# Score tiles and max tiles interleaved by row half in a causal attention kernel

## The chip, the cores and the metric

The kernel runs on one core of a Trainium2 chip. The metric is the device time of one execution in microseconds (us), of which three runs are shown; the profile is of one further execution.

## The reference

A transformer block on x of shape (4, 2048, 256), float32. Sixteen heads of 16 dimensions.

```python
x = x + attention(layernorm(x), Wq, Wk, Wv, Wo)   # rotary Q and K, causal softmax
x = x + ffn(layernorm(x), w1, b1, w2, b2)         # relu, width 1024

scores = einsum('bhqd,bhkd->bhqk', Q, K) / sqrt(16)
scores = where(causal_mask, -inf, scores)
attn = softmax(scores, axis=-1)
out = einsum('bhqk,bhkd->bhqd', attn, V)
```

## The kernel before

Three stages run one after the other. Stage 1 normalizes x, projects Q, K and V, applies the rotation, and stores Q and K as float16 high and low parts and V in scratch memory. Stage 3 scales the attention output, projects it, and runs the feed-forward net. Stage 2, the attention, is where the change lies.

Stage 2 works on 16 groups (4 batches x 4 groups of 4 heads; index `i`). A group has 40 steps (`STEPS`, L49): for each chunk `c` of 512 queries, the key blocks `kb` of 128 keys from 0 to the last that the causal mask leaves. The last four steps of a chunk touch the diagonal (`is_diagonal`, L62); the others, 0, 4, 8 and 12 in chunks 0 to 3, are the full steps, 24 per group. In each step, for each of the 4 heads of the group, a score tile of 128 keys x up to 512 queries is computed (`score_tile`, L716), ScalarE takes its exponential out of PSUM (L869), GpSimd zeroes what lies above the diagonal in diagonal steps (L899), and one step later TensorE multiplies the probabilities with V (`pv_step`, L726, in two parts of half the columns, each of four matmuls that use 32 columns of the array each, float32). ScalarE copies the output bank once per chunk, in the step after the chunk's last (L860); the first value matmul of the next chunk waits for that copy (L733).

The softmax needs each query's maximum before its scores. It is computed half a group of steps ahead (`LAG` = 20 steps, L58), by separate matmuls with queries on the partitions, the max tiles (`max_pair`, L692, matmul L705); VectorE reduces them to maxima. For a tile wholly below the diagonal, one reduce takes the two banks of a pair (L797). For a tile that crosses it, VectorE adds a mask and takes the maximum bank by bank (L804). When a chunk's tiles are through, VectorE makes the row of negated maxima (L812, L817, L822), which travels through scratch memory into the score operand. Every step carries one max tile per head; full steps carry full tiles, diagonal steps carry diagonal ones (`max_tiles`, L72). The last 20 steps of the last group have no max tiles left.

All these matmuls have a contraction of at most 64 rows. Heads 0 and 2 of a group lie in partitions 0 to 63, heads 1 and 3 in partitions 64 to 127 (`HROWS`), for scores and max tiles alike. Below, S0 to S3 and M0 to M3 are the score and max matmuls of heads 0 to 3.

TensorE's order in a step is written out by hand in `iteration` (L754): S0 S1, M0 M1, S2, value part 0, S3, M2 M3, value part 1. Scores use three PSUM banks in turn, so a score waits until ScalarE has read the third score before it (L720). Max tiles use four banks, one per head, so a pair waits until VectorE has read the same pair of the step before (L702, L704): by one wait for both banks, on the pair's first matmul, for a full tile. The value parts wait for all four exponentials of the step before (L737), or for all four of its masks (L735), and ScalarE's first exponential of a step waits for the value parts of two steps before (L866).

Of the kernel before, what the change touches and what calls it, by code (L numbers as in the profile page):

```python
# [46 lines left out]
NP = G // 2  # L47
# [14 lines left out]
def is_diagonal(s):  # L62
    c, kb = STEPS[s]
    return kb >= TPC * c


def diagonals(s):

    return sum(is_diagonal(t) for t in range(s))
# [455 lines left out]
def stage2(nc, x, qk_d, v_d, att_d, rows_d, rinv_d, weight_ds, weights, ops):  # L525
    with ExitStack() as ctx:
# [41 lines left out]
        STEPS_M = NIT * NS  # L568
# [7 lines left out]
        def m_use(t, j):  # L576

            return G * t + j

        def bank_of(use):  # L580

            return M_BANK + use % NM

        def s_bank(s, j):

            return S_BANK + (G * s + j) % SB

        def read_before(i, s, j):

            u = G * s + j  # L590
            last_in_bank = u - SB if u >= SB else max(t for t in range(ST) if t % SB == u) - ST
            return ST * i + last_in_bank + 1

        def crosses_diagonal(qt, kc):
            return kc == qt // TPC
# [93 lines left out]

        @block.tensor  # L690
        def _(pe):
            def max_pair(t, pair):  # L692

                p, use = t // NS % 2, m_use(t, 2 * pair)
                if pair == 0 and t % NS == 0:
                    pe.wait_ge(m_in[p], 128 * (t // NS // 2 + 1))
                qt, kc = MAX_TILES[t % NS]
                w = min(CH, (qt + 1) * P - kc * CH)
                for jj in range(2):
                    rows = slice(HROWS * jj, HROWS * (jj + 1))  # L700
                    if crosses_diagonal(qt, kc):
                        pe.wait_ge(m_read, use + jj + 1)  # L702
                    elif jj == 0:
                        pe.wait_ge(m_read, use + 2)  # L704
                    nc.tensor.matmul(ps[:, bank_of(use + jj), 0:w], mq[rows, p, pair, qt * P:(qt + 1) * P],  # L705
                                     mk[rows, p, pair, kc * CH:kc * CH + w], start=True, stop=True).then_inc(m_ready, 1)

            def filler_pair(p, s, pair):

                qt, kc = MAX_TILES[(s + LAG) % NS]  # L710
                for jj in range(2):
                    rows = slice(HROWS * jj, HROWS * (jj + 1))
                    nc.tensor.matmul(ps[:, M_BANK + 2 * pair + jj], mq[rows, p, pair, qt * P:(qt + 1) * P],
                                     mk[rows, p, pair, 0:CH], start=True, stop=True)

            def score_tile(i, p, s, j):  # L716

                c, kb = STEPS[s]
                q0 = max(0, kb - TPC * c) * P
                pe.wait_ge(p_done, G + read_before(i, s, j))  # L720
                rows = slice(HROWS * (j % 2), HROWS * (j % 2 + 1))
                nc.tensor.matmul(ps[:, s_bank(s, j), q0:CH], ak[rows, p, j // 2, kb * P:(kb + 1) * P],  # L722
                                 aq[rows, p, j // 2, c * CH + q0:(c + 1) * CH], start=True, stop=True
                                 ).then_inc(s_ready, 1)

            def pv_step(i, p, s, part):  # L726

                c, kb = STEPS[s]
                q0 = max(0, kb - TPC * c) * P
                half = (CH - q0) // 2  # L730
                if part == 0:
                    if kb == 0:
                        pe.wait_ge(o_copied, NC * i + c)  # L733
                    if is_diagonal(s):
                        pe.wait_ge(mask_done, G * (NDIAG * i + diagonals(s) + 1))  # L735
                    else:
                        pe.wait_ge(p_done, ST * i + G * s + G + G)  # L737
                cols = slice(q0 + half * part, q0 + half * (part + 1))
                for j in range(G):

                    last = nc.tensor.matmul(ps[32 * j:32 * j + 32, O_BANK, cols], v[:, p, kb, j, :],  # L741
                                            prob[:, s % 2, j, cols], start=kb == 0 and part == 0,
                                            stop=kb == TPC * (c + 1) - 1 and part == 1)
                if part == 1:
                    last.then_inc(pv_done, 1)

            def value_step(i, p, s, part):

                if s > 0:
                    pv_step(i, p, s - 1, part)  # L750
                elif i > 0:
                    pv_step(i - 1, 1 - p, NS - 1, part)

            def iteration(i, p, use):  # L754

                pe.wait_ge(a_in[p], A_DMAS * 16 * (use + 1))
                pe.wait_ge(v_in[p], 16 * (use + 1))
                for s in range(NS):
                    t = NS * i + s + LAG
                    if t == STEPS_M:  # L760
                        pe.wait_ge(m_read, NM + m_use(STEPS_M, 0))
                    if s in CHUNK_START:
                        pe.wait_ge(rows_in[STEPS[s][0]], 16 * ROWS_DMAS * (i + 1))
                    score_tile(i, p, s, 0)
                    score_tile(i, p, s, 1)
                    if t < STEPS_M:
                        max_pair(t, 0)
                    elif is_diagonal(s):
                        filler_pair(p, s, 0)
                    score_tile(i, p, s, 2)  # L770
                    value_step(i, p, s, 0)
                    score_tile(i, p, s, 3)
                    if t < STEPS_M:
                        max_pair(t, 1)
                    elif is_diagonal(s):
                        filler_pair(p, s, 1)
                    value_step(i, p, s, 1)

            for t in range(LAG):
                for pair in range(NP):  # L780
                    max_pair(t, pair)
            for u in range(NIT // 2):
                iteration(2 * u, 0, u)
                iteration(2 * u + 1, 1, u)
            pv_step(NIT - 1, 1, NS - 1, 0)
            pv_step(NIT - 1, 1, NS - 1, 1)
# [492 lines left out]
```

## Time and profile before

| | |
|---|---|
| median of 3 runs | 2129.21 us (2128.51 to 2129.35) |
| profiled execution | 2130.91 us, span 2129.2 us |
| mean granted TensorE clock | 0.973 of full speed |
| TensorE busy | 1996.2 us, 94% |
| VectorE busy | 1909.1 us, 90% |
| ScalarE busy | 1446.1 us, 68% |
| GpSimd busy | 637.3 us, 30% |

The span is the time from the first to the last instruction of the profiled execution. In the rows, PE is TensorE's matmuls, PEld its weight loads, DVE is VectorE, ACT ScalarE, POOL GpSimd. Busy time is a union: instructions that overlap on one engine count once, so a mean duration can be longer than the time from one start to the next.

### The profile page before, as it was taken

The page shows a single profiled execution, that of the slowest core. Times are in us where ns is not written, and L with a number is a line of the kernel's source. Part 1 is how long each engine was busy: PE and PEld are TensorE (multiplying, and loading weights), DVE is VectorE, ACT ScalarE, POOL GpSimd, SP SyncE. Part 2 cuts the span into 40 slices and gives each one's busy share as a digit, 9 for nine tenths or more (in the row PEclk, how much of TensorE's full clock was granted, in tenths as well). Part 3 has the DMA queues.
Part 4 walks back from the last instruction along what each step waited for, and adds up shares of the span by engine and source line. Part 5 has one row for each costly group of instructions (what it writes and reads, how often), then busy time and mean ns, then how long its engine had stood idle before and what let it go on. Part 6 is the DMA issues. An engine that isn't in the chain of part 4 may idle for free. (4 is left out here: it accounts for less than half of the span.)

```text
span 2129.2 us, 53450 instructions
## 1 busy us (share of the span) xinstructions
PE 1996.2 (94%) x19104; PEld 797.7 (37%) x19104; DVE 1909.1 (90%) x4039; ACT 1446.1 (68%) x3092; POOL 637.3 (30%) x1265
## 2 busy tenths in 40 slices
PE   5787499999999999999999999999999979999998
PEld 3444023232322223232232322323323246667776
DVE  8999799999999999999999999999999247777775
ACT  5665078888888888888888888888888823333222
POOL 7999512120222212121121211212212123333331
PEclk9999589999999999999999999999999989999999
DMA  5657430321303223031230313303030212222220
GB/s 178 219 207 212 149 61 23 78 43 41 68 22 78 36 49 67 18 78 35 55 67 18 75 30 63 67 18 68 28 62 18 66 44 83 93 85 86 82 84 26
DMA packets 133319, 153.17 MB, mean 72 GB/s; under 512 B 23904, under 2 KB 99424, under 8 KB 132832
## 3 DMA queue, kind: packets, MB, share of 16 engines
q1 hardware_dynamic: 133088, 150.19, 27.1%
q8 instruction: 132, 2.16, 0.4%
q14 instruction: 99, 0.81, 0.1%
HBM read 90.38 MB, written 59.77 MB: 71 GB/s over the span
## 5 line engine op out<-in xcount | busy, mean ns | idle before, releaser
L869 ACT ACTIVATE s_prob<-s_ps 128x512 f32<-128x512 f32 (+3 forms) x2560 | 1170.1, 542 | 245.5 <-PE s_ps L722 240.9
L797 DVE TENSOR_REDUCE s_part<-s_ps 128x2 f32<-128x1024 f32 x768 | 899.1, 1221 | 17.7 <-PE s_ps L705 3.9
L741 PE MATMUL s_ps<-s_prob,s_v 128*32 128x256 f32 (+3 forms) x10240 | 738.3, 360 | 10.2 <-ACT s_o L860 3.2
L722 PE MATMUL s_ps<-aq,ak 64*128 64x512 f16 (+3 forms) x2560 | 680.9, 353 | 8.1 <-ACT s_prob L869 1.5
L705 PE MATMUL s_ps<-mk,mq 64*128 64x512 f16 (+3 forms) x2560 | 604.1, 355 | 39.7 <-DVEq L841 17.6
L899 POOL TENSOR_SCALAR_AFFINE_SELECT s_prob<-s_prob 128x128 f32<-128x128 f32 x1024 | 286.5, 292 | 1130.4 <-ACT s_prob L869 1113.6
L804 DVE CUSTOM_DVE_ANT_0 s_ps<-s_ps,mask_sb 128x512 f32<-128x512 f32 (+3 forms) x1024 | 464.8, 529 | 4.0 <-PE s_ps L705 3.1
L722 PEld LDWEIGHTS s_ps<-aq,ak 64*128 64x128 f16 x2560 | 186.1, 93 | 535.2 <-ACT s_prob L869 464.7
L741 PEld LDWEIGHTS s_ps<-s_prob,s_v 128*32 128x32 f32 x10240 | 202.1, 108 | 446.3 <-issue 347.0
L705 PEld LDWEIGHTS s_ps<-mk,mq 64*128 64x128 f16 x2560 | 152.6, 94 | 89.3 <-DVE s_part L804 35.9
L1167 ACT ACTIVATE s_h_f<-s_ps,s_b_s 128x512 f32<-128x512 f32 x128 | 88.0, 687 | 105.8 <-PE s_ps L1032 84.8
L804 DVE DVE_READ_ACCUMULATOR2_ANT s_part<- 128x1 f32 x1024 | 146.5, 143 | 0.0
L1042 PE MATMUL s_ps<-w_hi,s_h_hi 128*128 128x256 f16 x512 | 139.6, 273 | 2.0 <-DVE s_h_lo L1107 2.0
L1042 PE MATMUL s_ps<-w_lo,s_h_hi 128*128 128x256 f16 x512 | 139.6, 273 | 0.0
L1042 PE MATMUL s_ps<-w_hi,s_h_lo 128*128 128x256 f16 x512 | 139.6, 273 | 0.0
L1107 DVE TENSOR_TENSOR s_h_lo<-s_h_f,s_h_hi 128x512 f16<-128x512 f32 x128 | 99.9, 781 | 4.4
L446 POOL TENSOR_TENSOR s_rot_b<-s_rot_b,s_sin 128x512 f32<-128x512 f32 x64 | 92.9, 1451 | 15.3 <-DVE s_rot_b L385 15.2
L141 POOL TENSOR_TENSOR o_in<-o_in,r_in 128x1024 f32<-128x1024 f32 x16 | 38.3, 2395 | 196.8 <-DMA r_in<-rinv_scratch 196.8
L448 POOL TENSOR_TENSOR s_rot_a<-s_rot_a,s_rot_b 128x512 f32<-128x512 f32 x64 | 93.7, 1464 | 5.0
L1105 DVE CAST s_h_hi<-s_h_f 128x512 f16<-128x512 f32 x128 | 61.8, 483 | 30.1 <-ACT s_h_f L1167 24.8
L322 PE MATMUL s_ps<-s_xt_hi,s_w_hi 128*128 128x512 f16 x128 | 43.2, 423 | 39.0 <-DVE s_xt_lo L377 34.6
L1032 PE MATMUL s_ps<-s_xt_hi,w_hi 128*128 128x512 f16 x256 | 77.0, 383 | 2.7 <-DVE s_xt_lo L1100 2.6
(88 smaller groups left out, 1561.1 us busy)
## 6 DMA issues: line engine op xcount, KB each, us to landing
v_scratch<-s_vst SPq DMA_DIRECT2D x32, 512.0 KB, 4.0
s_v<-v_scratch SPq DMA_DIRECT2D x16, 1024.0 KB, 12.0
att_scratch<-s_o SPq DMA_DIRECT2D x64, 256.0 KB, 2.5
aq<-qk_scratch SPq DMA_DIRECT2D x96, 128.0 KB, 4.2
ak<-qk_scratch SPq DMA_DIRECT2D x96, 128.0 KB, 6.9
s_xin<-x SPq DMA_DIRECT2D x16, 512.0 KB, 4.4
qk_scratch<-s_r_lo SPq DMA_DIRECT2D x64, 128.0 KB, 2.2
qk_scratch<-s_r_hi SPq DMA_DIRECT2D x64, 128.0 KB, 2.4
```

What stands on the lines that cost most here:

```text
L446: nc.gpsimd.tensor_tensor(rot_b[:, g], rot_b[:, g], sin[:, tok], ALU.mult).then_inc(rotsin_done, 1)
L448: nc.gpsimd.tensor_tensor(rot_a[:, g], rot_a[:, g], rot_b[:, g], ALU.add).then_inc(rot_done, 1)
L705: nc.tensor.matmul(ps[:, bank_of(use + jj), 0:w], mq[rows, p, pair, qt * P:(qt + 1) * P], mk[rows, p, pair, kc * CH:kc * CH + w], start=Tr ...
L722: nc.tensor.matmul(ps[:, s_bank(s, j), q0:CH], ak[rows, p, j // 2, kb * P:(kb + 1) * P], aq[rows, p, j // 2, c * CH + q0:(c + 1) * CH], st ...
L741: last = nc.tensor.matmul(ps[32 * j:32 * j + 32, O_BANK, cols], v[:, p, kb, j, :], prob[:, s % 2, j, cols], start=kb == 0 and part == 0, s ...
L797: nc.vector.tensor_reduce(part[:, qt // TPC, :, pair, qt % TPC, kc], ps[:, bank_of(use):bank_of(use) + 2, 0:w], AX.X, ALU.max).then_inc(m_ ...
L804: nc.vector.tensor_tensor_reduce(out=ps[:, bank, 0:w], in0=ps[:, bank, 0:w], in1=mask[:, CH - w:CH], scale=1.0, scalar=MASKED, op0=ALU.add ...
L869: nc.scalar.activation(prob[:, s % 2, j, q0:CH], ps[:, s_bank(s, j), q0:CH], ACT.Exp, scale=1.0 / (SQK * DK ** 0.5)).then_inc(p_done, 1)
L899: nc.gpsimd.affine_select(out=block, in_=block, compare_op=ALU.is_ge, fill=0.0, base=0, pattern=[[1, P]], channel_multiplier=-1).then_inc( ...
L1042: last = nc.tensor.matmul(ps[:, Y_BANK + pair, t * D:(t + 1) * D], a[:, p, k, tt * P:(tt + 1) * P], w[:, k], start=q == 0, stop=q == len(m ...
L1107: nc.vector.tensor_tensor(h_lo[:, p, f], h_f[:, f % 2], h_hi[:, p, f], ALU.subtract).then_inc(hlo_done, 1)
L1167: nc.scalar.activation(h_f[:, f % 2], ps[:, H_BANK + f % 2], ACT.Relu, bias=b1_s[:, f:f + 1], scale=SH / SQK).then_inc(h_done, 1)
```

## The change

In a step that is not diagonal and that still has max tiles, the order on TensorE becomes S0 M1, S1 M0, value part 0, S2 M3, S3 M2, value part 1. `max_pair` takes the heads to issue; the wait for both banks is on the first matmul of the pair that is issued, which is now the one in partitions 64 to 127, and the second needs no wait of its own. The other steps are issued as before.

```diff
             def max_pair(t, pair, heads=(0, 1)):
...
-                for jj in range(2):
+                for jj in heads:
                     rows = slice(HROWS * jj, HROWS * (jj + 1))
                     if crosses_diagonal(qt, kc):
                         pe.wait_ge(m_read, use + jj + 1)
-                    elif jj == 0:
+                    elif jj == heads[0]:
                         pe.wait_ge(m_read, use + 2)
...
                     if s in CHUNK_START:
                         pe.wait_ge(rows_in[STEPS[s][0]], 16 * ROWS_DMAS * (i + 1))
+                    if t < STEPS_M and not is_diagonal(s):
+                        for pair in range(NP):
+                            score_tile(i, p, s, 2 * pair)
+                            max_pair(t, pair, (1,))
+                            score_tile(i, p, s, 2 * pair + 1)
+                            max_pair(t, pair, (0,))
+                            value_step(i, p, s, pair)
+                        continue
                     score_tile(i, p, s, 0)
                     score_tile(i, p, s, 1)
                     if t < STEPS_M:
```

Called with `(1,)` and then `(0,)`, `heads[0]` is 1 and then 0, so each of the two matmuls of a full tile carries the wait for both banks; for the second it is the same value, which the first has already waited for.

## Rows read from the trace of the kernel before

**Rows 1.** The page, busy time of engines: us, share of the span, instructions
```profile
PE 1996.2 (94%) x19104; PEld 797.7 (37%) x19104; DVE 1909.1 (90%) x4039; ACT 1446.1 (68%) x3092; POOL 637.3 (30%) x1265
```
**Rows 2.** Busy time by stretch: from:to, length, each engine, granted clock, DMA
```profile
266.00:1580.00 1314.00, 1292.24 (x13972) 386.55 (x13973) 1287.87 (x2784) 1084.59 (x2388) 262.79 (x937) 0.99 0.25 50
...
1708.00:2129.20 421.20, 400.09 (x2851) 277.02 (x2850) 298.73 (x563) 127.62 (x198) 123.80 (x98) 0.98 0.22 74
```
**Rows 3.** In order of time, TensorE in one full step: start, us, engine, line
```profile
802.22 0.39 PE L722 MATMUL s_ps<-aq,ak 64*128 64x512 f16 x2
802.23 0.10 PEld L705 LDWEIGHTS s_ps<-mk,mq 64*128 64x128 f16 x2
802.45 0.38 PE L705 MATMUL s_ps<-mk,mq 64*128 64x512 f16 x2
...
802.66 0.38 PE L722 MATMUL s_ps<-aq,ak 64*128 64x512 f16 x1
...
802.97 0.64 PE L741 MATMUL s_ps<-s_prob,s_v 128*32 128x256 f32 x8
...
803.54 0.39 PE L722 MATMUL s_ps<-aq,ak 64*128 64x512 f16 x1
803.54 0.60 PE L705 MATMUL s_ps<-mk,mq 64*128 64x512 f16 x2
...
804.64 0.39 PE L722 MATMUL s_ps<-aq,ak 64*128 64x512 f16 x2
```
**Rows 4.** In order of time, VectorE and ScalarE around the same step
```profile
799.40 6.07 DVE L797 TENSOR_REDUCE s_part<-s_ps 128x2 f32<-128x1024 f32 x5
...
802.71 2.06 ACT L869 ACTIVATE s_prob<-s_ps 128x512 f32<-128x512 f32 x4 [0.36 <-PE s_ps L722]
```
**Rows 5.** VectorE behind a chunk's maxima, and those reduces' durations, min/median/max ns
```profile
821.40 4.61 DVE L797 TENSOR_REDUCE s_part<-s_ps 128x2 f32<-128x1024 f32 x4
...
L797 DVE TENSOR_REDUCE s_part<-s_ps x4: 1216/1216/1219, 821.4 to 824.8; 128x2 f32<-128x1024 f32 x4
```
**Rows 6.** VectorE in order of time, runs of reduces: chunks 1, 2, 2, 3
```profile
821.40 9.38 DVE L797 TENSOR_REDUCE s_part<-s_ps 128x2 f32<-128x1024 f32 x8
...
748.61 12.11 DVE L797 TENSOR_REDUCE s_part<-s_ps 128x2 f32<-128x1024 f32 x10 [0.26 <-PE s_ps L705]
...
761.09 7.00 DVE L797 TENSOR_REDUCE s_part<-s_ps 128x2 f32<-128x1024 f32 x6
...
776.71 28.77 DVE L797 TENSOR_REDUCE s_part<-s_ps 128x2 f32<-128x1024 f32 x24
```
**Rows 7.** VectorE at the end of chunk 1's diagonal steps
```profile
837.15 0.33 DVE L804 CUSTOM_DVE_ANT_0 s_ps<-s_ps,mask_sb 128x128 f32<-128x128 f32 x1
...
837.40 0.14 DVE L804 DVE_READ_ACCUMULATOR2_ANT s_part<- 128x1 f32 x1
...
838.36 4.84 DVE L797 TENSOR_REDUCE s_part<-s_ps 128x2 f32<-128x1024 f32 x4 [0.26 <-PE s_ps L705]
```
**Rows 8.** TensorE, max matmuls that waited for the reduce begun at 821.40
```profile
822.68 0.39 PE L705 MATMUL s_ps<-mk,mq 64*128 64x512 f16 x2
```
**Rows 9.** The second step of chunk 2, in order of time
```profile
840.22 0.39 PE L722 MATMUL s_ps<-aq,ak 64*128 64x512 f16 x1
840.49 2.12 ACT L869 ACTIVATE s_prob<-s_ps 128x512 f32<-128x512 f32 x4
...
840.69 0.64 PE L741 MATMUL s_ps<-s_prob,s_v 128*32 128x256 f32 x8
...
841.26 0.39 PE L722 MATMUL s_ps<-aq,ak 64*128 64x512 f16 x1
...
842.37 0.39 PE L722 MATMUL s_ps<-aq,ak 64*128 64x512 f16 x2
```
**Rows 10.** The first step of chunk 2: masks of the step before, scores 0 and 1
```profile
837.02 1.02 POOL L899 TENSOR_SCALAR_AFFINE_SELECT s_prob<-s_prob 128x128 f32<-128x128 f32 x4 [0.39 <-ACT s_prob L869]
...
837.62 0.39 PE L722 MATMUL s_ps<-aq,ak 64*128 64x512 f16 x2
```

More of the change, by code:

```diff
@@ L691, in _, with max_pair @@
         def _(pe):
-            def max_pair(t, pair):
+            def max_pair(t, pair, heads=(0, 1)):
                 p, use = t // NS % 2, m_use(t, 2 * pair)
```

## The prediction, made before the changed kernel was run

> **What bounds the kernel now.** I read the page's busy times first, then the table of stretches, then the attention stretch in order of time, TensorE and VectorE against each other. The page has TensorE at 94% and VectorE at 90% of the span [rows 1]; the stretch from 266 to 1580 us, in which score steps and max tiles run together, is 62% of the span, and there TensorE is busy 1292 and VectorE 1288 of 1314 us, ScalarE only 1085, at a granted clock of 0.99, the 2.4 GHz level [rows 2]. Two engines at 98% say nothing on which waits for the other. The order of time does. A full step in its steady state runs from 802.22 to 804.64, 2.42 us, and TensorE's sequence in it has no hole [rows 3]: scores 0 and 1 start together at 802.22 (one in each half of the array's rows), max tiles 0 and 1 together at 802.45, score 2 alone at 802.66, the first value part at 802.97, score 3 with max tile 2 at 803.54, max tile 3 alone behind them, then the second value part, and at 804.64 the next step. So a pair of 64-row matmuls, or one alone, takes a slot of 0.22 to 0.23; the last slot ahead of a value part 0.31 (802.66 to 802.97); a value part 0.57 (802.97 to 803.54). There are five slots, 3 x 0.22 + 2 x 0.31 + 2 x 0.57 = 2.42, which is the step.
>
> VectorE's five reduces in the same stretch take 6.07 us, the last of them 1.22 to its end, so (6.07 - 1.22)/4 = 1.21 from start to start, twice that being 2.42 again [rows 4]. Left to itself it is faster: right behind a chunk's maxima, where max tiles lie ready, four reduces take 4.61 us, so (4.61 - 1.22)/3 = 1.13 [rows 5]. That is 2.26 us per full step. TensorE therefore bounds full steps, by 2.42 against 2.26, and VectorE's holes hide in the reduces' durations, not in the idle column. ScalarE needs 2.06 us per step and idles 0.36 [rows 4].
>
> **What the change does to TensorE.** No instruction is added or removed in a full step: four scores, four max tiles, two value parts, the same waits, no DMA. Only the order moves, and it applies where max tiles remain: 24 full steps x 16 groups less the last group's 12 of the last chunk = 372 of 640. Old slots: (S0,S1) (M0,M1) (S2) V (S3,M2) (M3) V. New ones: (S0,M1) (S1,M0) V (S2,M3) (S3,M2) V. Each letter pair now has one matmul in each half of the rows, so one slot of 0.22 goes: TensorE's floor becomes 2 x (0.23 + 0.31 + 0.57) = 2.21. That a score and a max tile do run side by side is seen at 803.54 [rows 3]; that a second matmul of the same half follows 0.22 to 0.23 behind the first, its load already done beneath it, is seen at 802.23 and 802.45, where the loads of both max tiles lie under scores 0 and 1. What bounds the price of the new order from both sides: at best the whole slot (-0.22), at worst nothing, should the pairs not form; I take the whole slot, since each new adjacency has a row.
>
> The Trainium skill ("TensorE: Matmul & The Clock Gate", section "Part 3: Packing small matmuls") says otherwise of the load: weights load beneath a running matmul only when the row group differs, though its text also allows the background buffer. In the new order score 1 follows max tile 1 in the same half, twice a step. The loads at 802.23 stand against the strict reading; its result is a rival below.
>
> **What is late next.** With 2.21 on TensorE, VectorE's 2.26 is the bound, if tiles come in time. Let reduce A start at 0: its two banks are free at 1.22, and a waiting max matmul starts 0.06 later (reduce from 821.40 to 822.62, matmul at 822.68) [rows 5, 8]. Max tile 1 starts at 1.28, max tile 0 one slot later at 1.51, ends 0.38 later at 1.89 (that duration from [rows 3]), and a reduce starts up to 0.2 behind it (the first pair's matmuls end at 802.83, the reduce that takes them begins, by the mean spacing, at 799.40 + 3 x 1.21 = 803.03): 2.09, needed at 2.26. The half-step on TensorE is 1.11 against 1.13, so it waits 0.02 to 0.03 at each max tile and keeps pace.
>
> Added waits: score 1 is now queued behind the wait of max tile 1, score 3 behind that of max tile 3, and score 2 behind the first value part, which waits for the four exponentials of the step before. The ring is value part, 0.57, score 2, 0.49 to its exponential (802.22 to 802.71), two exponentials (1.03 to 1.12, from 2.06 for four that overlap), 0.06 to the next value part: 2.15 to 2.24 [rows 3, 4]. Below 2.26, by little; this is the tightest cover in the forecast, and it sets the upper end. In the first full step after a diagonal the value part also waits for GpSimd's masks: they end at 838.04 and the value part would come at 837.62 + 0.53 = 838.15 [rows 10]; covered by 0.1. In the second step of a chunk the value part waits for the copy of the outputs; score 2, at 840.22 before, is issued behind it at 841.26, but ScalarE is then busy until about 841.5 with two exponentials begun at 840.49, and score 2's could start at 841.75: some 0.3 late, hidden because it must only end by the value part of the following step, about 842.9. TensorE leaves that step at 842.37 as before [rows 9]. So this step gains nothing.
>
> **The sum.** A run of n reduces at VectorE's own pace takes 1.131 (n - 1) + 1.22 (1.131 is (4.61 - 1.216)/3 to the third digit). Against the runs of one group [rows 6]:
> - chunk 1, 8 reduces: 9.38 against 9.14, 0.24, x 16 = 3.8;
> - chunk 2, 10 and 6 reduces: 12.11 against 11.40 and 7.00 against 6.88, together 0.83, less 0.2 for the step that waits for the copy, x 16 = 10.1;
> - chunk 3, 24 reduces: 28.77 against 27.23, 1.54, x 15 = 23.1.
>
> That is 37.0 us. At the ends of the runs of chunks 1 and 3 the time from the last reduce to the first masked tile is held as the others are; I take 0.05 of the 1.21 - 1.13 = 0.08, x 31 = 1.6. Diagonal steps keep their order and their time, but TensorE enters them earlier against VectorE, by about 0.2 (reduces now start some 0.25 later relative to TensorE's step than before, less what the old order's later second pair costs). Behind chunk 1's diagonal VectorE is starved: four masked tiles 0.25 apart would from 837.15 be through at 837.90, and the next reduce starts at 838.36, 0.46 late [rows 7]; 0.2 of it returns, x 16 = 3.2. Behind chunk 3 it is starved by under 0.1; I count 1. Sum 37.0 + 1.6 + 3.2 + 1 = 43 us. Stage 1, stage 3 (421 us, [rows 2]) and the last 20 steps, which have no max tiles, are untouched.
>
> The profiled execution took 2130.9 (span 2129.2), so 2088; the median of the runs shown is 1.7 lower, so 2086.
>
> **Rivals.**
> - Half the gain: the ring through ScalarE, or small waits on both sides, settles full steps at about 2.34. For: the ring's upper reading is 0.02 from VectorE's pace, and TensorE's slack per half is 0.02 to 0.03. Against: all its terms are measured. Half of 43 gives 2107.
> - The strict load rule: 0.09 for one load shown twice per step gives 2.21 + 0.18 = 2.39; 37 us at 0.16 per step are some 230 steps bound by TensorE, 0.03 on each is 7 us, 2122. Against it the loads of [rows 3].
> - No pairing, or a bound I don't see that stands at 2.42: 2129. Against it the free pace of [rows 5].
> - Slower: the max wait ahead of score 1 together with score 2 behind the value part starves ScalarE. Place: the second step of each chunk, where the exponentials come 0.3 late [rows 9], three times per group, 47 times: +14 us, 2143. It decides once the lateness isn't absorbed before the next value part (room about 0.05 us) and full steps give nothing back, that is if the ring is over 2.42. The ring's terms speak against it.
>
> **How the numbers follow.** Full gain 0.67 (its own range 2080 to 2094), half 0.13, load rule 0.06, none 0.07, slower 0.07. 0.2% of this kernel is 4.3 us, about what a measurement can tell from no change; the load rule's 7 us lies beyond it. So faster 0.85 (with a little taken off the last), same 0.08, slower 0.07. The range 2079 to 2110 holds the first two cases and leaves out the rest; its lower end is some 7 us more than the sum, should more of the holes at diagonals close.
>
> **What would show it.** Full steps of 2.26 from score 0 to score 0; reduces 1.13 apart throughout the runs (24 of them in 27.2 to 27.4 us instead of 28.77); score 0 and max tile 1 starting within some 0.03; ScalarE's idle time per step split in two holes. Wrong would be: max tile 0 starting over 0.3 behind max tile 1 (loads exposed), the value part idle before it with ScalarE as releaser (the ring), or a stage between 266 us and the last reduce that isn't 40 to 45 us shorter.

## The result, and the profile after

The changed kernel takes 2095.48 us (median of 4, 2091.61 to 2099.28) against 2128.86 for the kernel before on the same chip: a ratio of 0.9842, 95% interval [0.9829, 0.9854], 33 us less, with 2086 forecast. On another chip the same kernel came to 0.9815 [0.9801, 0.9828] (2091.58 against 2130.11), 38.5 us less. The profiled execution took 2093.28 us, 37.6 less than the profiled one of before, where the sum said 43.

The stretches, as from:to, length, each engine's busy time, clock and DMA; the third holds the last 20 steps, the fourth stage 3:

```profile
266.00:1540.00 1274.00, 1239.35 (x13941) 369.85 (x13941) 1258.78 (x2772) 1108.69 (x2383) 261.63 (x933) 1.00 0.26 52
1540.00:1626.00 86.00, 82.49 (x940) 24.52 (x938) 85.10 (x186) 74.17 (x160) 17.02 (x61) 1.00 0.05 16
1626.00:1668.00 42.00, 40.99 (x424) 11.97 (x420) 0.36 (x2) 36.76 (x81) 12.95 (x32) 1.00 0.26 83
1668.00:2091.50 423.50, 402.43 (x2842) 278.10 (x2840) 291.62 (x563) 127.11 (x195) 123.16 (x97) 0.97 0.21 73
```

Against [rows 2] TensorE's busy share of the first stretch fell from 98.3% to 97.3%, VectorE's rose from 98.0% to 98.8%. The shares hardly tell. The order of time does; TensorE (PE) in the steady state, which answers to [rows 3]:

```profile
780.18 0.39 PE L722 MATMUL s_ps<-aq,ak 64*128 64x512 f16 x1
780.21 0.10 PEld L705 LDWEIGHTS s_ps<-mk,mq 64*128 64x128 f16 x2
780.21 0.57 PE L705 MATMUL s_ps<-mk,mq 64*128 64x512 f16 x2
780.22 0.10 PEld L722 LDWEIGHTS s_ps<-aq,ak 64*128 64x128 f16 x1
780.44 0.38 PE L722 MATMUL s_ps<-aq,ak 64*128 64x512 f16 x1
...
780.74 0.64 PE L741 MATMUL s_ps<-s_prob,s_v 128*32 128x256 f32 x8
...
781.31 0.39 PE L722 MATMUL s_ps<-aq,ak 64*128 64x512 f16 x1
...
782.44 0.39 PE L722 MATMUL s_ps<-aq,ak 64*128 64x512 f16 x1
```

From 780.18 to 782.44 a full step takes 2.26. Score 0 starts, max tile 1 follows 0.03 later (its wait for VectorE), score 1 comes at 780.44, the value part at 780.74, 0.30 later, and the second half begins 0.57 after that. Four slots and two waits of 0.03. (A value part is four float32 matmuls in the program and eight records, x8, in the rows; its matmuls use all 128 rows of the array.) VectorE (DVE) in runs of reduces, one group of chunks 1 and 2, and chunk 3 (answering to [rows 6]):

```profile
717.85 9.14 DVE L807 TENSOR_REDUCE s_part<-s_ps 128x2 f32<-128x1024 f32 x8
...
734.50 3.49 DVE L807 TENSOR_REDUCE s_part<-s_ps 128x2 f32<-128x1024 f32 x3 [0.33 <-PE s_ps L705]
...
738.15 8.01 DVE L807 TENSOR_REDUCE s_part<-s_ps 128x2 f32<-128x1024 f32 x7 [0.16 <-PE s_ps L705]
...
746.53 6.82 DVE L807 TENSOR_REDUCE s_part<-s_ps 128x2 f32<-128x1024 f32 x6
...
761.96 27.24 DVE L807 TENSOR_REDUCE s_part<-s_ps 128x2 f32<-128x1024 f32 x24
```

9.14 for 8 and 27.24 for 24 are VectorE's own pace to 0.01 us, (27.24 - 1.22)/23 = 1.131. The one hole left within a run is in chunk 2 at 738.15 (some 0.26 in all), the step that waits for the copy of the outputs, as forecast. The bound has moved from TensorE's slots to VectorE's reduces.

### The profile page after: what moved, and what is told of

Same layout as the page of the kernel before. It is cut to its first block and busy times, and to the rows that moved or that the text cites. A ratio compares the mean times of both kernels' runs of the same rounds, so it can differ in the third digit from the quotient of the medians.

```text
span 2091.5 us, 53450 instructions
## 1 busy us (share of the span) xinstructions
PE 1944.1 (93%) x19104; PEld 781.3 (37%) x19104; DVE 1874.4 (90%) x4039; ACT 1473.9 (70%) x3092; POOL 636.9 (30%) x1265
## 5 line engine op out<-in xcount | busy, mean ns | idle before, releaser
L879 ACT ACTIVATE s_prob<-s_ps 128x512 f32<-128x512 f32 (+3 forms) x2560 | 1198.3, 537 | 177.3 <-PE s_ps L722 145.1
L807 DVE TENSOR_REDUCE s_part<-s_ps 128x2 f32<-128x1024 f32 x768 | 875.1, 1219 | 7.4 <-PE s_ps L705 7.1
L705 PE MATMUL s_ps<-mk,mq 64*128 64x512 f16 (+3 forms) x2560 | 680.6, 356 | 52.4 <-DVE s_part L807 21.2
L722 PE MATMUL s_ps<-aq,ak 64*128 64x512 f16 (+3 forms) x2560 | 714.1, 351 | 5.2 <-ACT s_prob L879 2.3
L722 PEld LDWEIGHTS s_ps<-aq,ak 64*128 64x128 f16 x2560 | 176.1, 93 | 489.6 <-ACT s_prob L879 459.1
L705 PEld LDWEIGHTS s_ps<-mk,mq 64*128 64x128 f16 x2560 | 166.2, 93 | 124.1 <-DVE s_part L807 50.7
L814 DVE DVE_READ_ACCUMULATOR2_ANT s_part<- 128x1 f32 x1024 | 154.3, 151 | 0.0
L1171 ACT CAST s_xt_hi<-s_ps 128x512 f16<-128x512 f32 x32 | 17.2, 589 | 89.7 <-PE s_ps L1032 89.7
```

Of the source, the lines that this page charges most:

```text
L807: nc.vector.tensor_reduce(part[:, qt // TPC, :, pair, qt % TPC, kc], ps[:, bank_of(use):bank_of(use) + 2, 0:w], AX.X, ALU.max).then_inc(m_ ...
L814: nc.vector.tensor_tensor_reduce(out=ps[:, bank, 0:w], in0=ps[:, bank, 0:w], in1=mask[:, CH - w:CH], scale=1.0, scalar=MASKED, op0=ALU.add ...
L879: nc.scalar.activation(prob[:, s % 2, j, q0:CH], ps[:, s_bank(s, j), q0:CH], ACT.Exp, scale=1.0 / (SQK * DK ** 0.5)).then_inc(p_done, 1)
```

## The experiments

Ratios are to the kernel before on the chip of that run, with 95% intervals.

**Which part of the new order gains?** e1 keeps pairs of their own and only moves score 2 behind the first value part. e4 does the rest alone: it interleaves the first half and leaves score 2 ahead.

```diff
 e1, full steps, in place of the interleaved lines:
+score_tile(i, p, s, 2 * pair)
+score_tile(i, p, s, 2 * pair + 1)
+max_pair(t, pair)
+value_step(i, p, s, pair)
 e4, full steps:
+score_tile(i, p, s, 0)
+max_pair(t, 0, (1,))
+score_tile(i, p, s, 1)
+max_pair(t, 0, (0,))
+score_tile(i, p, s, 2)
+value_step(i, p, s, 0)
+score_tile(i, p, s, 3)
+max_pair(t, 1)
+value_step(i, p, s, 1)
```

> Full steps issue S0 S1, M0 M1, value part 0, S2 S3, M2 M3, value part 1: score and max pairs stay pairs of their own, only score 2 moves behind the first value part. Theory (slots: the gain comes from an even count of 64-row matmuls on each side of a value part, whoever is paired with whom): four slots as in the changed kernel, full step 2.26, stage 2 about 40 us shorter than before, time 2090 to 2097. Rival (the gain comes from pairing a score with a max tile): as before, 2125 to 2131, full step 2.42.

> Full steps issue S0 M1 S1 M0 S2, value part 0, S3 M2 M3, value part 1: the interleaving in the first half step, but score 2 stays ahead of the value part. Slot theory: five slots as before, full step 2.42, time 2127 to 2132. Rival (interleaving itself gains): half the gain, 2105 to 2115.

e1: 2094.05 us, ratio 0.9826 [0.9812, 0.9839]. e4: 2129.71, 0.9996 [0.9987, 1.0005]. So the whole gain comes from moving score 2 behind the first value part, and none from the interleaving that the change is described by. VectorE in e4, chunks 1 and 3, has the times of [rows 6]:

```profile
909.70 9.38 DVE L810 TENSOR_REDUCE s_part<-s_ps 128x2 f32<-128x1024 f32 x8
...
954.80 28.77 DVE L810 TENSOR_REDUCE s_part<-s_ps 128x2 f32<-128x1024 f32 x24
```

To see whether interleaving costs or gains a little, the changed kernel and e1 ran again side by side.

> The changed kernel itself, on one chip with e10 and e11. Theory (who is paired with whom is of no account): the same as e10 within 0.1%, 2091 to 2097. Rival (the wait for max tile 1 ahead of score 1 costs something): 2 us or more above e10.

> e1 again, on the same chip as e9: 2091 to 2097, equal to e9 within 0.1% by the theory, 2 us or more below it by the rival.

e9: 2091.58, 0.9815 [0.9801, 0.9828]. e10: 2093.31, 0.9823 [0.9809, 0.9836]. The rival wanted the changed kernel 2 us or more above; it is 1.7 below. That lies inside both intervals, and the wait ahead of score 1 shows no cost.

**Does a pair have to be made by the order?** e2 follows each score with the max tile of its own 64 rows: S0 M0 S1 M1, value part, S2 M2 S3 M3, value part.

```diff
-max_pair(t, pair, (1,))
+max_pair(t, pair, (0,))
 score_tile(i, p, s, 2 * pair + 1)
-max_pair(t, pair, (0,))
+max_pair(t, pair, (1,))
```

> As the changed kernel, but each score is followed by the max tile of its own 64 rows (S0 M0 S1 M1, S2 M2 S3 M3). Slot theory: M0 waits for S0's half, S1 starts with M0, M1 behind: three slots per half step, 2 x (0.23 + 0.22 + 0.31 + 0.57) = 2.65 us per full step, 0.39 over VectorE's 2.26, x 372 = some 110 us over before's 2129 less what is hidden: 2200 to 2225. Rival (the order within a half step doesn't matter, only that score 2 left the first half): 2090 to 2100.

2095.50 us (two executions), 0.9836 [0.9818, 0.9854], level with the changed kernel: my slot theory, in the form that only neighbours in the program pair up, missed by 100 us. TensorE in e2, in order of time:

```profile
780.39 0.41 PE L722 MATMUL s_ps<-aq,ak 64*128 64x512 f16 x2
780.40 0.10 PEld L705 LDWEIGHTS s_ps<-mk,mq 64*128 64x128 f16 x1
780.41 0.09 PEld L722 LDWEIGHTS s_ps<-aq,ak 64*128 64x128 f16 x1
780.42 0.10 PEld L705 LDWEIGHTS s_ps<-mk,mq 64*128 64x128 f16 x1
780.61 0.40 PE L705 MATMUL s_ps<-mk,mq 64*128 64x512 f16 x2
...
780.94 0.64 PE L741 MATMUL s_ps<-s_prob,s_v 128*32 128x256 f32 x8
...
781.51 0.39 PE L722 MATMUL s_ps<-aq,ak 64*128 64x512 f16 x2
...
781.74 0.38 PE L705 MATMUL s_ps<-mk,mq 64*128 64x512 f16 x2
```

Program order is S0 M0 S1 M1. The weight loads keep to it (780.40 for M0, 780.41 for S1, 780.42 for M1), but both scores run from about 780.39 and both max tiles from about 780.61: S1 started 0.2 us ahead of M0, which stands before it. The two halves of the rows behave as two streams, and what counts between two value parts is how many matmuls the fuller half has. Before: scores 0 and 2 and max tile 0 in the lower half against score 1 and max tile 1, so 3; then 2 (score 3 and max tile 3 against max tile 2). Five. In e1, e2 and the change: 2 and 2. In e4: 3 and 2. That rule fits all five orders. "Neighbours in the program pair up" gives the same counts for four of them; e2 alone tells the two apart, and there it gives six slots, against the four that were found.

**What bounds each kernel?** Reduces of full tiles read half the columns; the other half is left out of the maxima.

```diff
-ps[:, bank_of(use):bank_of(use) + 2, 0:w], AX.X, ALU.max
+ps[:, bank_of(use):bank_of(use) + 2, 0:w // 2], AX.X, ALU.max
```

> The kernel before, but VectorE's reduces of full max tiles read half the columns (the other half is left out of the maxima), some 0.55 us less each. Theory (TensorE bounds full steps of the kernel before by its five slots): full steps stay at 2.42, and only the stretches where VectorE was behind a diagonal gain: 2112 to 2129. Rival (VectorE bounds them): some 0.5 us or more less per full step, under 2000.

> The changed kernel with the same halved reduces. Theory (its full steps are bound by VectorE at 2.26, with TensorE's four slots next at 2.21 and the ring through ScalarE at 2.15 to 2.24): full steps of 2.21 to 2.24, which is 56 to 67 us below the same edit on the kernel before, so some 2055 to 2070. Rival (TensorE or ScalarE already bounds the changed kernel): 2088 to 2097, as without the edit.

e5: 2115.50, 0.9926 [0.9910, 0.9943]. e6: 2059.49, 0.9660 [0.9644, 0.9676]: 56.0 apart. VectorE in e5, then in e6:

```profile
950.97 0.69 DVE L797 TENSOR_REDUCE s_part<-s_ps 128x2 f32<-128x512 f32 x1 [0.59 <-PE s_ps L705]
952.10 0.69 DVE L797 TENSOR_REDUCE s_part<-s_ps 128x2 f32<-128x512 f32 x1 [0.44 <-PE s_ps L705]
953.39 0.69 DVE L797 TENSOR_REDUCE s_part<-s_ps 128x2 f32<-128x512 f32 x1 [0.59 <-PE s_ps L705]
```

```profile
981.60 0.69 DVE L807 TENSOR_REDUCE s_part<-s_ps 128x2 f32<-128x512 f32 x1 [0.41 <-PE s_ps L705]
982.71 0.69 DVE L807 TENSOR_REDUCE s_part<-s_ps 128x2 f32<-128x512 f32 x1 [0.41 <-PE s_ps L705]
983.82 0.69 DVE L807 TENSOR_REDUCE s_part<-s_ps 128x2 f32<-128x512 f32 x1 [0.41 <-PE s_ps L705]
```

With reduces of 0.69, VectorE waits for TensorE before each of these. In e5 the step is still 953.39 - 950.97 = 2.42, and the runs of 24 and of 10 reduces take as long from first to last start as before (27.54 and 10.88), so the 15.7 us that e5 gains lie outside full steps (9.0 of it in the very first 24 reduces, which run before any score): TensorE bounded the full steps of the kernel before. In e6 it is 983.82 - 981.60 = 2.22 (2.213 over a run): TensorE's four slots, 2 x (0.23 + 0.31 + 0.57) = 2.22. The ring through ScalarE, which I put at 2.15 to 2.24, doesn't lengthen even that. So the change freed 0.21 per full step, and VectorE's pace lets 0.16 of it be seen.

**Why not in diagonal steps too?** e3 uses e1's order wherever max tiles remain; e11 adds only the first diagonal step of chunks 1 to 3.

```diff
-if t < STEPS_M and not is_diagonal(s):
+if t < STEPS_M:                                                  # e3
+if t < STEPS_M and s > 0 and not is_diagonal(s - 1) or t < STEPS_M and not is_diagonal(s):   # e11
```

> As e1, but in the diagonal steps too, so long as max tiles remain. Slot theory: diagonal steps lose a slot of 0.07 to 0.22 each on TensorE, so VectorE is starved less behind the diagonals of chunk 1: the remaining holes are some 0.3 us per group, so 3 to 6 us less than e1. Rival (diagonal steps are bound by VectorE throughout): the same as e1 within 1 us. If the value part behind scores 2's place now waits for the masks of GpSimd, up to 5 us slower than e1.

> e1 with the new order also in the first diagonal step of chunks 1 to 3, whose value parts wait for exponentials and not for masks. TensorE's part of that step gets 0.2 shorter, but its masks come later, and the value part of the second diagonal step waits for them (in e3 that was at 3.12 us after the step's start, in e1 at 3.06). By the ring theory no gain: e10 within 2 us, if anything slower by 1 to 3. Rival (the lead on TensorE counts): 3 us below e10.

e3: 2118.57, 0.9943 [0.9930, 0.9957], 24 us above e1 where I expected up to 5 at worst. e11: 2091.66, 0.9818 [0.9805, 0.9831], 1.7 us below e10 and not told apart from it: neither a gain of 3 us nor a loss is seen. TensorE, ScalarE and GpSimd (POOL) in e3, over two diagonal steps:

```profile
1004.57 0.29 POOL L908 TENSOR_SCALAR_AFFINE_SELECT s_prob<-s_prob 128x128 f32<-128x128 f32 x1 [0.19 <-ACT s_prob L878]
...
1004.91 0.64 PE L741 MATMUL s_ps<-s_prob,s_v 128*32 128x256 f32 x8 [0.38 <-POOL s_prob L908]
...
1005.48 0.34 PE L722 MATMUL s_ps<-aq,ak 64*128 64x384 f16 x2
...
1005.85 1.67 ACT L878 ACTIVATE s_prob<-s_ps 128x384 f32<-128x384 f32 x4 [0.52 <-PE s_ps L722]
...
1006.50 0.67 POOL L908 TENSOR_SCALAR_AFFINE_SELECT s_prob<-s_prob 128x128 f32<-128x128 f32 x2 [0.72 <-ACT s_prob L878]
...
1007.23 0.53 PE L741 MATMUL s_ps<-s_prob,s_v 128*32 128x192 f32 x8 [0.36 <-POOL s_prob L908]
```

A ring: the value part at 1004.91 waited for the last mask (1004.57 + 0.29), scores 2 and 3 queue behind it to 1005.48, their exponentials follow, their masks, and the next value part, at 1007.23, again waits for the masks: 2.32 us from one to the other. In e1, where score 2 is issued ahead of the value part in these steps, the same two value parts start at 992.48 and 994.48, 2.00 apart. e7 and e8 take the masks out (left out of the computation; the value parts then wait for the exponentials), of e3 and of e1:

```diff
-if is_diagonal(s):
-    pe.wait_ge(mask_done, G * (NDIAG * i + diagonals(s) + 1))
-else:
-    pe.wait_ge(p_done, ST * i + G * s + G + G)
+pe.wait_ge(p_done, ST * i + G * s + G + G)
...
-if is_diagonal(s):
-    mask_step(i, s)
```

> e3 (own pairs in diagonal steps too) without GpSimd's masks, which are left out; the value parts wait for the exponentials alone. Theory (e3's 24 us come from a ring in diagonal steps: value part, score 2 behind it, its exponential, masks, next value part): they go, and the time is that of e8 or a few us less, 2085 to 2096. Rival (diagonal steps are slower for the shorter spread of max tiles, or for something on VectorE): still 15 us or more above e8.

> The control of e7: e1 (own pairs in full steps alone) without GpSimd's masks. Masks are hidden in e1, so 2086 to 2094. If they were on the path there too, clearly under 2085.

e7: 2090.10, 0.9809 [0.9792, 0.9825]. e8: 2091.64, 0.9811 [0.9795, 0.9828]. Without masks e3's order costs nothing and gains nothing that can be told; with them it costs 24 us. The ring through the masks is its cause. e8's ratio is level with e10's on another chip, so masks are hidden when the order is kept to full steps.

## Why the prediction was right, and where its sum was too large

**Direction and mechanism held.** TensorE had bound full steps (e5), one slot went, VectorE's 1.131 took over (27.24 for 24 reduces), the copy step kept its hole, waits on max tiles are 0.03, the ring through ScalarE stays under VectorE's pace. The rivals of half the gain, no pairing and slower fell with the 2.26 step. The strict load rule fell too: in [rows 3] and in the rows after, a half's second matmul follows 0.23 behind its first, its load already done beneath it (780.21 and 780.22 in the changed kernel), and e6's step of 2.21 lies under that rule's 2.39.

**The reason given for the lost slot was half wrong.** I wrote that each letter pair has one matmul in each half and so one slot goes. Pairing by letters is not needed (e2), and pairing a score with a max tile gains nothing by itself (e1, e4): the balance of the halves between value parts decides. Both ways of counting give four slots for this change, so it was luck that the reason did not matter here, and the change's time alone could not have told them apart. (The floor of 2.21 in the prediction is 2.22 by its own terms; e6 measured 2.213.)

**The sum: 43 forecast, 37.6 between the profiled executions.** Three terms were mis-sized.
- Runs of reduces: 37.0 forecast, 35.2 found, by the time from first to last start of all 47 runs (10 and 6 of chunk 2 taken as one). Chunk 3 was nearly right: 22.8, not 23.1. In chunk 2 I had read an untypical group: of its 16 runs 14 took 18.15 from first to last start, mine 18.26. Mine gained the forecast 0.63, the typical one 0.53; the found sum is 9.1, not 10.1. In chunk 1 two of 16 runs already ran at VectorE's pace: 3.3, not 3.8.
- The stretches between runs: 5.8 forecast, 3.9 found. The ends of runs gave 1.8 (1.6 forecast) and chunk 3's diagonals 2.1 (1 forecast), of which 1.2 came in the first group alone. The 0.2 at chunk 1's diagonal, 3.2 in all, did not come. VectorE at that place in the changed kernel, answering to [rows 7]:

```profile
995.39 0.35 DVE L814 CUSTOM_DVE_ANT_0 s_ps<-s_ps,mask_sb 128x128 f32<-128x128 f32 x1
995.64 0.16 DVE L814 DVE_READ_ACCUMULATOR2_ANT s_part<- 128x1 f32 x1
996.13 1.23 DVE L807 TENSOR_REDUCE s_part<-s_ps 128x2 f32<-128x1024 f32 x1 [0.33 <-PE s_ps L705]
```

The last masked tile would be through at 995.64, the reduce starts at 996.13: 0.49 late, against 0.46 before. TensorE came to the diagonal earlier and did not keep its lead. From 380 to 1500 us max matmuls waited 26.1 us for masked reads, 20.3 before, which fits a lead spent at the banks; I ran nothing on it.

- What follows the reduces was taken as untouched. Its work is, its clock isn't the same in each execution. The last 21.5 us of the span, after and then before:

```profile
2070.00:2091.50 21.50, 16.20 (x114) 11.73 (x112) 6.47 (x11) 2.75 (x4) 0.00 (x0) 0.92 0.07 26
```

```profile
2107.70:2129.20 21.50, 16.16 (x122) 11.62 (x120) 7.90 (x14) 3.44 (x5) 0.00 (x0) 1.00 0.07 26
```

A clock of 0.92 there is 3.4 us at the 1.2 GHz level, 1.7 us lost. The changed kernel is 39.3 us ahead at the last full reduce, 40.5 at stage 3's first matmul (in the steps without max tiles the kernel before had the lower clock, 0.96 against 1.00), 39.3 again from 1746 us of the kernel before on, and 37.7 at the end. So 1.6 of the shortfall goes with the clock of these two executions.

**The rest, from the profiled execution to the median.** The forecast put the median 1.7 us under the profiled execution; it came out 2.2 above it. Executions of the changed kernel spread from 2088.4 to 2099.3 in nine, those of before on the same two chips from 2128.3 to 2131.6. On the first chip the longer had the lower mean clock: 0.974 with 2091.6 and 2093.3, 0.970 with 2097.7, 0.968 with 2099.3. The last two have no trace. e9's profiled execution, 2.9 us longer in span than the first one, shows such a place, the scores without max tiles at the end of stage 2:

```profile
1600.00:1668.00 68.00, 65.54 (x674) 18.25 (x672) 27.55 (x53) 58.58 (x123) 15.71 (x41) 0.97 0.17 57
```

The same window stood at 1.00 in the first profile. Whether the shorter step makes such dips more frequent, or they fall by chance, stays open. The point was 9 us low, and 2095.48 lies just outside the 2080 to 2094 that I gave the full gain. My range held because it reached to half the gain, which was put there for another case than the one that came.

## What to carry to other kernels

For matmuls that use half of the array's rows, count per half between two instructions that need all of it, and balance the counts; the order of the two halves' instructions among each other was of no account here. When two engines read 98% busy, halve the work of one: if the step stays as it was (here 2.42 in e5), that engine was not the bound. And an order that is right for one kind of step can close a ring in another (here value part, score, exponential, mask), so follow what is queued behind each wait before extending it. Before multiplying a run's excess by its count, read several of them.

## What the runs showed of the hardware

A matmul in one 64-row half started 0.2 us ahead of one that stands before it in the program and uses the other half (e2, both scores from about 780.39, the max tiles from 780.61). The changed kernel shows the same by 0.03 us: its two max tiles of 0.38 take 0.57 from 780.21, so max tile 0 starts at about 780.40, ahead of score 1 at 780.44. I had expected starts in program order. The Trainium skill ("TensorE: Matmul & The Clock Gate", section "Part 3: Packing small matmuls") says matmuls start and end strictly in program order; the measurement differs, for halves of 64 rows.
